# Edge stage of a graph network kernel: groups of six whole buckets in place of 512 slots

## The reference

```python
h = relu(layernorm(x))
x = x + hypergraph_conv(relu(hypergraph_conv(h)))      # four hops over the edges
h = relu(layernorm(x))
edge_in = concat([h[src], h[dst], edge_weight1], axis=1)
e = silu(silu(edge_in @ eW1 + eb1) @ eW2 + eb2)        # 412,500 x 128
agg = segment_sum(e, src)
x = x + (silu(concat([h, agg]) @ nW1 + nb1) @ nW2 + nb2)
```

## Time and profile before

| what | value |
|---|---|
| median of 3 runs | 9404.6 us |
| profiled execution | 9440.02 us |
| its span, first to last instruction | 9438.3 us |
| edge stage in it (first matmul to the node stage's first load) | about 6169 to 9279 us |
| tables in it | about 5979 to 6160 us |
| TensorE, VectorE, ScalarE, GpSimd busy over the span | 91%, 82%, 57%, 32% |
| granted clock of TensorE over the span | 0.971 |

### The profile page before, as it was taken

How to read it: one execution, slowest core, us unless ns; L and a number is a source line. 1 busy time by engine, 2 the same in 40 slices (tenths; PEclk the granted TensorE clock), 3 DMA queues, 4 the chain that set the end, 5 groups by cost and what they waited for, 6 DMA issues and landing times. The chain is left out here.

```text
span 9438.3 us, 289390 instructions
## 1 busy us (share of the span) xinstructions
PE 8612.8 (91%) x95106; PEld 7671.8 (81%) x95890; DVE 7764.0 (82%) x21596; ACT 5345.2 (57%) x14224; POOL 2984.4 (32%) x4177
## 2 busy tenths in 40 slices
PE   3999999999999989998888999589999999999997
PEld 2777777777777779998888898489888988889885
DVE  8999999999999985775888786478888888888884
ACT  3777777777777760000777776245555555555552
POOL 5877777777777740000000000011111111111110
PEclk9999999999999999998999999599999999999998
DMA  3666666666666677764999998433333333333333
GB/s 76 145 146 145 147 147 146 148 147 145 145 146 145 146 159 197 191 190 108 229 222 211 239 239 190 108 108 96 92 93 96 91 98 89 98 91 97 92 96 72
DMA packets 1475615, 1312.44 MB, mean 139 GB/s; under 512 B 829933, under 2 KB 1211095, under 8 KB 1473637
## 3 DMA queue, kind: packets, MB, share of 16 engines
q1 hardware_dynamic: 1444438, 1270.13, 56.0%
q0 software_dynamic: 28224, 26.62, 1.1%
q10 hardware_dynamic: 1840, 0.53, 0.0%
HBM read 777.40 MB, written 361.77 MB: 121 GB/s over the span
## 5 line engine op out<-in xcount | busy, mean ns | idle before, releaser
L621 POOL TENSOR_SCALAR OH<-iot,kd 128x102 bf16<-128x102 bf16 x3440 | 2359.7, 704 | 148.0 <-PE S L753 146.7
L2169 POOL DMA_INDIRECT Qx<-tab_q,tidx x294 | 404.5, 1376 | 5249.2 <-DVE skt L2203 2607.2
L1424 PE MATMUL wp<-AF,XS 128*128 128x256 f32 x9604 | 1214.5, 285 | 159.7 <-issue 112.0
L1424 PEld LDWEIGHTS wp<-AF,XS 128*128 128x128 f32 x9604 | 1166.1, 191 | 190.8 <-issue 190.4
L911 ACT ACTIVATE RB<-PS 128x256 int16<-128x256 f32 x2401 | 898.4, 380 | 721.1 <-PE PS L779 669.5
L1450 ACT ACTIVATE AF<-RG 128x1536 fp32r<-128x1536 uint8 x686 | 1022.6, 1491 | 342.7 <-PE wp L1424 201.9
L794 PE MATMUL HP<-T3a,RB 128*128 128x193 bf16 x9604 | 1189.2, 246 | 10.2 <-ACT RB L911 9.3
L753 PE MATMUL S<-LH,OHf 128*102 128x256 f32 (+14 forms) x6860 | 1157.1, 316 | 39.6 <-ACT LH L875 17.5
L2190 ACT ACTIVATE Z<-Zb 128x512 f32<-128x512 f32 x882 | 556.2, 631 | 985.9 <-DVE Zb L2248 981.0
L875 ACT ACTIVATE LH<-LB,pl 128x128 f32<-128x128 bf16 (+14 forms) x4116 | 1112.8, 356 | 0.3 <-DVE LB L981 0.2
L753 PEld LDWEIGHTS S<-LH,OHf 128*102 128x102 f32 x6860 | 921.0, 169 | 175.1 <-issue 86.9
(11 more groups left out here) (329 smaller groups left out, 16069.1 us busy)
## 6 DMA issues: line engine op xcount, KB each, us to landing
RG<-adjT SPq DMA_DIRECT2D x1372, 224.0 KB, 7.0
adj<-RB SPq DMA_DIRECT2D x343, 448.0 KB, 2.8
adjT<-RT SPq DMA_DIRECT2D x686, 224.0 KB, 3.7
RG<-adj SPq DMA_DIRECT2D x686, 224.0 KB, 4.8
sdb<-bk SPq DMA_DIRECT2D x196, 768.0 KB
sdb<-bk SPq DMA_DIRECT2D x98, 384.0 KB
sdb<-bk SPq DMA_DIRECT2D x98, 261.0 KB
WR<-wk SPq DMA_DIRECT2D x882, 9.0 KB
```

The lines of the kernel that those rows point to most:

```text
L621: ins = e.tensor_scalar(OH[:, g * GT + k, :], iot1[:, 0:KEYS], kd[:, g * GT + k:g * GT + k + 1], None, ALU.is_equal)
L1424: ins = e.matmul(ps[b][:, 0:256], lhsT=XS[:, n * PB + m, :, :].rearrange("p c f -> p (c f)"), rhs=AF[:, (b + n) % 3, m, :], start=n == 0 a ...
```

## The change

The group is no longer 512 slots but GW = 504 = 6 x 84, except the last, which keeps 512: 84 regular, 144 for self loops, 284 late. SLOTS = 8 x 504 + 512 = 4544, NX = 284, in NXT = 4 tiles of XT = 71. A group's four tiles begin TW = 126 slots apart and are still 128 wide: the second layer takes `Y` at 0, 126, 252 and 378, so 506 columns are computed (`wide`), and the two columns that a tile has beyond its 126 are given no source row, since `skt` (the source numbers by tile, turned to `sk`) has zeros there. Each piece of `sdb` and `WR` has PLN = 1520 slots, at a step of 1512. The pieces of a group are six whole buckets; the last group has one.

```diff
-SLOTS = 4608
+GW = 6 * SLB
+NGB = 9
+TW = GW // 4
+SLOTS = (NGB - 1) * GW + 512
 NX = SLOTS - AT_X
-NXT = 3
+NXT = 4
 XT = NX // NXT
...
-NTL = SLOTS // P
+NTL = NGB * 4
...
-            PWD = GPP * 512
+            PWD = GPP * GW
+            PLN = PWD + 512 - GW
...
-            sdb = [sbt(cx, f"sdb{n}", [P, 2, PWD], bf16) for n in range(3)]
-            WR = [sbt(cx, f"WR{n}", [P, PWD], bf16) for n in range(3)]
+            sdb = [sbt(cx, f"sdb{n}", [P, 2, PLN], bf16) for n in range(3)]
+            WR = [sbt(cx, f"WR{n}", [P, PLN], bf16) for n in range(3)]
...
+            def wide(g):
+
+                return 512 if g % GB9 == GB9 - 1 else GW + P - TW
+
+            def tile_at(t, g):
+
+                return t * (P if g % GB9 == GB9 - 1 else TW)
...
             def buckets_of(g):
 
-                at = g % GB9 * 512
-                return [(c,) + span(c * SLB, c * SLB + SLB, g) for c in range(at // SLB, min(NCH, (at + 511) // SLB + 1))]
+                c = g % GB9 * 6
+                return [(t,) + span(t * SLB, t * SLB + SLB, g) for t in range(c, min(NCH, c + 6))]
...
-                                e.dma_start(skt[q][0:NTL, :], bk[DS(k, 1), 0, :].rearrange("a (t n) -> (a t) n", n=P)).then_inc(l_sd[q], 16)
+                                e.dma_start(skt[q][0:NTL - 4, 0:TW], bk[DS(k, 1), 0, 0:SLOTS - 512].rearrange("a (t n) -> (a t) n", n=TW)).then_inc(l_sd[q], 16)
+                                e.dma_start(skt[q][NTL - 4:NTL, :], bk[DS(k, 1), 0, SLOTS - 512:SLOTS].rearrange("a (t n) -> (a t) n", n=P)).then_inc(l_sd[q], 16)
...
-                            e.matmul(pT[g % 2][:, :], lhsT=WB[:, :], rhs=WR[j][:, at:at + 512], start=True, stop=True)
+                            e.matmul(pT[g % 2][:, 0:wide(g)], lhsT=WB[:, :], rhs=WR[j][:, at:at + wide(g)], start=True, stop=True)
...
-                                e.matmul(o[:, :], lhsT=Pb[q][:, c, :], rhs=S_[:, :], start=False, stop=True, skip_group_check=True)
+                                e.matmul(o[:, 0:wide(g)], lhsT=Pb[q][:, c, :], rhs=S_[:, 0:wide(g)], start=False, stop=True, skip_group_check=True)
...
-                                ins = e.matmul(p2[g % 2][:, t * P:(t + 1) * P], lhsT=Y[g % 2][:, t * P:(t + 1) * P], rhs=nW["eW2s"][:, :],
+                                ins = e.matmul(p2[g % 2][:, t * P:(t + 1) * P], lhsT=Y[g % 2][:, tile_at(t, g):tile_at(t, g) + P], rhs=nW["eW2s"][:, :],
...
-                            e.activation(Y[g % 2][:, :], pT[g % 2][:, :], ACT.Silu, bias=nW["eb1s"][:, 0:1]).then_inc(l_y, 1)
+                            e.activation(Y[g % 2][:, 0:wide(g)], pT[g % 2][:, 0:wide(g)], ACT.Silu, bias=nW["eb1s"][:, 0:1]).then_inc(l_y, 1)
...
-                            ins = e.tensor_scalar(OsT[g % 2][:, :], v[:, 0, at:at + 512], pio[:, 0:1], None, ALU.is_equal)
+                            ins = e.tensor_scalar(OsT[g % 2][:, 0:wide(g)], v[:, 0, at:at + wide(g)], pio[:, 0:1], None, ALU.is_equal)
```

More of the change, by code:

```diff
@@ L2027, in piece_of @@
                 r = g % GB9
-                return r // GPP, r % GPP * 512
+                return r // GPP, r % GPP * GW
+            def wide(g):
+                return 512 if g % GB9 == GB9 - 1 else GW + P - TW
+            def tile_at(t, g):
+                return t * (P if g % GB9 == GB9 - 1 else TW)
             def first(g):
@@ L2038, in span @@
             def span(a, b, g):
-                at = g % GB9 * 512
-                return max(a - at, 0), min(b - at, 512)
+                at = g % GB9 * GW
+                return a - at, b - at
             def buckets_of(g):
-                at = g % GB9 * 512
-                return [(c,) + span(c * SLB, c * SLB + SLB, g) for c in range(at // SLB, min(NCH, (at + 511) // SLB + 1))]
+                c = g % GB9 * 6
+                return [(t,) + span(t * SLB, t * SLB + SLB, g) for t in range(c, min(NCH, c + 6))]
             def regular(g):
-                return min(512, AT_D - g % GB9 * 512)
+                return min(GW, AT_D - g % GB9 * GW)
             with nc.Block() as block:
@@ L2067, in turn @@
                                 e.dma_start(Qb[q][:, :, :], tab_q3[DS(i * (2 * P) + q * P, P), :].rearrange("p (c h) -> p c h", c=3)).then_inc(l_pl[q], 16)
-                                e.dma_start(skt[q][0:NTL, :], bk[DS(k, 1), 0, :].rearrange("a (t n) -> (a t) n", n=P)).then_inc(l_sd[q], 16)
+                                e.dma_start(skt[q][0:NTL - 4, 0:TW], bk[DS(k, 1), 0, 0:SLOTS - 512].rearrange("a (t n) -> (a t) n", n=TW)).then_inc(l_sd[q], 16)
+                                e.dma_start(skt[q][NTL - 4:NTL, :], bk[DS(k, 1), 0, SLOTS - 512:SLOTS].rearrange("a (t n) -> (a t) n", n=P)).then_inc(l_sd[q], 16)
                             done(e, l_p, i, (q - 1) * GB9 + (n + 1) * GPP - 1)
-                            b, t0, t1 = n, n * PWD, (n + 1) * PWD
+                            b, t0, t1 = n, n * PWD, min(n * PWD + PLN, SLOTS)
                             s = l_rec[n]
                             if n < 2:
-                                e.dma_start(sdb[b][:, :, :], bk[DS(k, 1), :, t0:t1].to_broadcast([P, 2, PWD])).then_inc(s, 16)
+                                e.dma_start(sdb[b][:, :, :], bk[DS(k, 1), :, t0:t1].to_broadcast([P, 2, PLN])).then_inc(s, 16)
                             else:
-                                e.dma_start(sdb[b][:, 0, :], bk[DS(k, 1), 0, t0:t1].to_broadcast([P, PWD])).then_inc(s, 16)
+                                e.dma_start(sdb[b][:, 0, :], bk[DS(k, 1), 0, t0:t1].to_broadcast([P, PLN])).then_inc(s, 16)
                                 e.dma_start(sdb[b][:, 1, 0:AT_D - t0], bk[DS(k, 1), 1, t0:AT_D].to_broadcast([P, AT_D - t0])).then_inc(s, 16)
@@ L2111, in stage_t @@
                             if g % GB9 == 0:
-                                e.wait_ge(l_sd[q], i * 16 + (16 if g >= 0 else 0))
+                                e.wait_ge(l_sd[q], i * 32 + (32 if g >= 0 else 0))
                                 e.wait_ge(l_sk, i * 2 + (q + 1 if g >= 0 else q - 1))
@@ L2223, in onehot @@
                                 ins = e.tensor_scalar(OdT[g % 2][:, h, 0:wd], v[:, 1, at:at + wd], pio[:, h:h + 1], None, ALU.is_equal)
-                            if wd < 512:
+                            if wd < GW:
                                 a, b = span(AT_D, AT_X, g)
```

## The result

| | kernel before | changed kernel |
|---|---|---|
| median (4 runs each, same chip) | 9404.4 us | 9602.5 us (9593.4 to 9614.4) |
| ratio, 95% interval | | 1.0208 [1.019, 1.0226] |
| span of the profiled execution | 9438.3 us | 9591.5 us |
| granted clock of TensorE over the span | 0.971 | 0.963 |
| tables: `tidx` issued to the edge stage's first weight load | 190.4 us | 302.5 us |

The account below looks back on a forecast made before the run. The edge stage was taken to go at TensorE's pace. 89 us from its matmuls plus 9 us at the tables made 98 us off 9404.6, so 9307 us, own range 9291 to 9325, with 8 in 10 for 9285 to 9342.

Parts of the forecast that it names:

- TensorE's only sizeable idle is 'issue' ... the change leaves that alone: Edge stage: TensorE idles 30.4 us in 41 pieces per 100 us view's waits, where the loop body ends; taken as unchanged.
- Nothing if the DMA splits badly over 71 partitions: Tables' row-number DMA: lower bound of its 9 us saving, set at zero; upper bound 15.4 us.
- The saving on TensorE's list: Edge stage: fewer and narrower matmuls save 0.91 us a block (0.82 to 1.01), 89 us over 98 blocks.
- 0.87 from distances: Edge stage: start-to-start matmul distances price 16 parts at 2.68 us, 8 whole buckets at 1.81; 0.87 us a block saved.
- 0.71 from whole groups: Edge stage: timing whole groups from first L2124 to next L2142 gives 0.71 us a block net for merging parts.
- the two small terms: Edge stage, per block: 506 columns for 512 save 0.06 us; narrower late-slot matmuls save 0.05 us.
- 506 columns and the late slots: Edge stage: narrower matmuls save 0.06 us a block; late matmuls 34 ns apart save 0.05, or 0.08 at 31 ns.
- VectorE's margin: Edge stage: OdT ends 0.95 us before TensorE needs it, falling to 0.85 (0.36 in the shortest turn); no wait appears.
- The weight loads of `Y` at odd starts: Second layer: 48 loads a block at new byte offsets could slow; 517 us if each load doubled; 4% with other TensorE surprises.
- Four gathers a block: GpSimd in the edge stage: four gathers for three, a block ahead and covered by its waits; cost nothing.
- The 9 us at the tables: Tables: 6,272 fewer packets in the row-number DMA shorten ScalarE's 15.40 us wait by 9.4 us, counted as 9.
- the one on the slower side: Second layer: odd-start weight loads of Y slow TensorE, 9824 us if loads double; 4%, other TensorE surprises included.

Follow-up runs that it names:

- the repaired kernels: Changed kernel with 64 idle TensorE instructions ahead of the edge loop and row-number DMA split in two, 9295.6 us; and b_pad132_split, 9389.4 us.
- a_pad64_xt92: Changed kernel with 64 idle TensorE instructions ahead of the edge loop and three late tiles of 92 slots for four of 71: 9296.1 us, ratio 0.9868 to before.
- a_xt70: Changed kernel with late tiles of 70 slots in place of 71, loop not moved: 9424.8 us.
- a_split: Changed kernel with the row-number DMA split in two, rows 0 to 63 and 64 to 70: 9465.0 us.
- b_pad132_split: Kernel before with 132 idle TensorE instructions ahead of the edge loop and row-number DMA split into rows 0 to 111 and 112 to 115: 9389.4 us, ratio 0.9975.
- b_pad64: Kernel before with 64 idle TensorE instructions ahead of the edge loop: 9461.2 us.
- a_pad32: Changed kernel with 32 idle TensorE instructions ahead of the edge loop: 9696.7 us.
- a_pad64_xt70: Changed kernel with 64 idle TensorE instructions ahead of the edge loop and late tiles of 70 slots for 71: 9440.5 us, ratio 1.002 to before.

## Why the prediction was wrong, by its steps

- **"TensorE's only sizeable idle is 'issue' ... the change leaves that alone": this step failed**, for 138 us. The 30.4 us in 41 pieces were read as the price of a jump at the end of the loop body. They were the visible part of a refetch of nine pieces in each turn, and its visible part depends on where the body lies and how it is timed. The change removed 181 instructions from the body and moved its start, and stayed at nine; the length was no longer at fault (7.2 pieces lie within eight from most places), the place was. The evidence was there before the change, in a view that wasn't read: between 6300 and 9200 us the kernel before moves 413 instruction packets, nine in each turn of the loop.
- **"Nothing if the DMA splits badly over 71 partitions": this step failed too**, for 112 us where 9 were to be gained. The risk was named, and its lower end was put at zero. Nothing in the trace excluded a loss. What the transfer takes on one engine, 27,832 elements at 1700 in 10 us, is 164 us, and SyncE's queue, the first `tab_p` store and ScalarE stand behind all of it.
- The clock had no term in the prediction. With the longer stops came 78.5 us at 0.50 in the changed kernel's edge stage, where the kernel before has none. They are part of the 138 us.
- The saving on TensorE's list held in kind and was mis-sized a little: 0.78 us a block between the repaired kernels, 0.83 by median turns, forecast 0.91 (0.82 to 1.01). Two readings stood there for the merging: 0.87 from distances, 0.71 from whole groups. The second, with the two small terms, gives 0.82. Distances between equal matmuls overstated the removed parts here; that whole groups contain their transitions would explain it, and wasn't tested. 506 columns and the late slots came as forecast: twelve of 71 columns in 0.55 us, with one duration of 0.208 off, are 31 ns apart, the better end.
- The rule from the Trainium skill ("TensorE: Matmul & The Clock Gate", "Back-to-back issue gap") would have made 45 fewer pairs worth 357 us, an estimate by that page; the repaired kernels differ by 75.6 us in the stage.
- VectorE's margin held nearly everywhere: TensorE waited for `OdT` 7 times, 2.3 us in all, in the changed kernel (once, 0.5 us, before), and once and for 1.2 us at most in the kernels with both repairs. The weight loads of `Y` at odd starts cost nothing: eight L2155 matmuls take 1.05 us as before. Four gathers a block stay hidden; GpSimd still waits 2126 us for TensorE.
- The 9 us at the tables came true where the DMA kept four engines: 190.4 us before, 180.3 in `a_pad64_xt92`. Spreading it wider, in `a_xt70` and `a_split`, gave no more (181.0 and 183.2).
- The rivals: the one on the slower side was a mechanism on TensorE that didn't exist. The real losses sat in the two things for which the prediction had a sentence and no price. With both put right, the time is 9295.6 and 9296.1, inside the range of 9285 to 9342, but that is partly luck: the repair also takes away the 44 us of gaps that the kernel before had, and which the forecast never counted. Like for like, against `b_pad132_split`, the edge stage gives 75.6 us where 80 to 99 were forecast.

## What to carry to other kernels

Ahead of a change to a long unrolled loop, look at the instruction queue in the stretch of the loop: packets in every turn mean that the body is being refetched, and "issue" gaps there are no constant; a few idle instructions ahead of the loop, or a shorter body, can be worth more than the change itself. When a tile's row count changes, ask what it divides by: a prime number of rows left a DMA of single elements at a quarter of its pace. And bound an unknown from both sides; a named risk with a price of zero is a forecast that it can't happen.

## What the runs showed that was not expected

- The changed kernel's loop body brings nine pieces of 16.4 KB in every turn (404 packets in 45 turns), and next to none (10 packets) when it lies 64 instructions further: 3149.9 against 2972.6 us. Nine pieces touched against eight fits all eight placements tried. Whether eight is a limit for other engines and programs wasn't tried.
- What such a refetch costs depends on the place: 1.8 us a block in the changed kernel and 2.8 with the same body 32 instructions further (3149.9 and 3250.3 us against 2972.6); 0.45 and 0.41 for the kernel before and `b_pad64`.
- In an edge stage with stops of 1 to 2 us TensorE's granted clock fell to 0.50 around some of them: for 78.5 us of the changed kernel's stage and 232.1 of `a_pad32`'s. In the kernel before, whose stops have a median of 0.75 us, it never fell there.
- DMAs of single elements moved 170, 510 and 668 packets per us for 71, 69 and 116 rows, which fits about 170 for each of 1, 3 and 4 engines, the largest divisors of the row counts up to 16.
- Gathers of 70 and 112 rows came with a stop in every block, in which TensorE and ScalarE both stand (1.3 us in one turn of `a_pad64_xt70`), in the two kernels whose loop had been moved: 142 and 95 us in all over the stage. In `a_xt70`, with the loop where it was, the same gathers brought none. What the engines wait for stays open.
